# Summing the field products of a tile with two row reductions instead of a tree of six adds

## The reference

```
e = stack of 39 lookups                      # (512, 39, 16), x0 = xk = e
for W in (f0, f1, f2):                       # (39*39, 128), (128*39, 128), (128*39, 128)
    z   = einsum('bfd,bgd->bfgd', x0, xk)    # all products of a field of x0 with a field of xk
    cur = einsum('bpd,pm->bmd', z, W)        # 128 maps
    outs.append(cur); xk = cur
h = concat(sum of each cur over d, dense_ctx)      # 3*128 + 16 numbers
h = relu(h @ W_top1 + b1); h = relu(h @ W_top2 + b2); y = h @ W_top3
```

## Time and profile before

| what | value |
|---|---|
| timed runs | 721.77, 726.46, 728.2 us (median 726.46) |
| profiled execution, its own time (first to last instruction) | 726.1 us |
| PE busy | 686.6 us, 95% |
| DVE busy | 614.4 us, 85% |
| ACT busy | 498.4 us, 69% |
| POOL busy | 255.3 us, 35% |

### The profile page before, as it was taken

One profiled execution on the slowest core, in us unless ns is written; L12 is line 12 of the kernel. 1 busy time (PEld: TensorE's weight loads), 2 busy tenths in 40 slices (PEclk: granted clock), 3 DMA queues, 4 the chain that ended last, 5 costly groups with the idle time before them and its releaser, 6 DMA issues.

```text
span 726.1 us, 12749 instructions
## 1 busy us (share of the span) xinstructions
PE 686.6 (95%) x3569; PEld 495.2 (68%) x3569; DVE 614.4 (85%) x1410; ACT 498.4 (69%) x1663; POOL 255.3 (35%) x247
## 2 busy tenths in 40 slices
PE   3769899999999999999999899999999999999998
PEld 0347567667677877766777687766677787777777
DVE  1638899999999866999999676899999986899990
ACT  2136678778786656878786545877878665787882
POOL 5655628137511707126710702415841000111020
PEclk9969999999999999999999989999999999999999
DMA  7181030303020210202111120020303020030000
GB/s 220 10 278 34 7 86 5 90 2 84 14 75 15 49 46 5 76 14 58 41 52 39 25 65 12 22 71 3 94 4 89 1 63 28 1 89 1 0 2 2
DMA packets 23425, 33.99 MB, mean 47 GB/s; under 512 B 7816, under 2 KB 10616, under 8 KB 22967
## 3 DMA queue, kind: packets, MB, share of 16 engines
q1 hardware_dynamic: 18230, 31.84, 14.4%
q0 software_dynamic: 5120, 1.29, 2.0%
HBM read 9.13 MB, written 0.00 MB: 13 GB/s over the span
## 4 chain that ended last, share of the span: by engine, by line
PE 55%; DVE 21%; issue 11%; ACT 2%; DVEq 1%
DVE sums L683 10%; PE x_ps L920 8%; PE v_ps L776 7%; PE v_ps L778 6%; PE v_ps L777 6%; PE a_ps L776 5%; PE a_ps L778 5%; PE a_ps L777 5%; PE s_ps L890 4%; PE s_ps L979 3%; DVE scaled L626 2%; ACT scaled L452 2%; DVE scaled L616 1%; DVE z_sb L656 1%; DVE sums L672 1%
## 5 line engine op out<-in xcount | busy, mean ns | idle before, releaser
L452 ACT ACTIVATE scaled<-a_ps,x0c 128x128 f32<-128x128 f32 x1216 | 350.3, 379 | 144.0 <-PE a_ps L778 135.8
L683 DVE SCALAR_TENSOR_TENSOR sums<-v_ps,x0c,sums 128x128 f32<-128x128 f32 x768 | 214.8, 341 | 38.4 <-PE v_ps L778 38.4
L776 PE MATMUL v_ps<-w_hi,x_hi 128*128 128x512 f32 x320 | 177.8, 556 | 9.1 <-DVE e_parts L574 4.7
L394 POOL DMA_INDIRECT e_sb<-in_tables,ids_now x140 | 165.6, 1183 | 47.3 <-issue 37.3
L410 POOL TENSOR_TENSOR diag_sb<-x0c,eye_sb 128x320 f32<-128x320 f32 x64 | 61.9, 967 | 329.0 <-PE s_ps L979 328.7
L778 PE MATMUL v_ps<-w_hi,x_lo 128*128 128x512 f32 x320 | 127.6, 399 | 0.0
L777 PE MATMUL v_ps<-w_lo,x_hi 128*128 128x512 f32 x320 | 127.5, 398 | 0.0
L776 PE MATMUL a_ps<-w_hi,x_hi 128*128 128x512 f32 (+1 forms) x320 | 124.5, 389 | 0.0
L777 PE MATMUL a_ps<-w_lo,x_hi 128*128 128x512 f32 (+1 forms) x320 | 123.7, 387 | 0.0
L778 PE MATMUL a_ps<-w_hi,x_lo 128*128 128x512 f32 (+1 forms) x320 | 123.5, 386 | 0.0
L920 PE MATMUL x_ps<-z_sb,w_sb 117*128 117x512 f32 (+1 forms) x210 | 109.5, 602 | 5.9 <-DVE z_sb L656 5.8
(11 more groups left out here) (110 smaller groups left out, 644.9 us busy)
## 6 DMA issues: line engine op xcount, KB each, us to landing
b_sb<-a_sb SPq DMA_DIRECT2D x300, 78.0 KB
w_sb<-in_w SPq DMA_DIRECT2D x1, 2496.0 KB
e_sb<-in_tables,ids_now POOLq DMA_INDIRECT x140
s_sb<-in_w SPq DMA_DIRECT2D x2, 1024.0 KB, 5.3
wt_sb<-in_wt SPq DMA_DIRECT2D x1, 768.0 KB
s_sb<-in_w SPq DMA_DIRECT2D x1, 512.0 KB, 10.5
wt_sb<-in_wt SPq DMA_DIRECT2D x1, 512.0 KB
w_raw<-in_w0a SPq DMA_DIRECT2D x1, 409.5 KB
```

The lines of the kernel that those rows point to most:

```text
L394: pool.indirect_dma_start(out=e_sb[0:rows, i, :], out_offset=None, in_=tables, in_offset=bass.IndirectOffsetOnAxis(ap=ids_now[0:rows, 0, i ...
L452: last = nc.scalar.activation(scaled[:, s % 2, to, j, :], bank[:, j * MAPS:(j + 1) * MAPS], ACT.Copy, scale=x0c[:, k % 4, s, lo + j:lo + j ...
L683: nc.vector.scalar_tensor_tensor(out=sums[:, s % 2, j, :], in0=v_ps[n % 2][:, j * MAPS:(j + 1) * MAPS], scalar=x0c[:, k % 4, s, lo + j:lo ...
L776: nc.tensor.matmul(to, high, w_high, start=True, stop=False)
```

## The change

`scaled` and `sums` become one buffer, `prods`, of 28 rows of 128 maps (for each of two tiles in turn). Rows 0 to 10 hold ACT's products of its last three groups, row 11 an intermediate sum, rows 12 to 15 the four partial sums that DVE accumulates, and rows 16 to 27 ACT's products of the first three groups. The old buffers had 24 and 4 rows, so the size is the same.

The six adds of `sum_tile` go. In their place stand two reductions over rows. `sum_early` runs at group position 4 of the tile itself, and sums rows 12 to 27 (16 rows) into row 11. `sum_late` runs at group position 0 of the next tile, behind line 672, and sums rows 0 to 11 (12 rows) into `x2t`. Both read the buffer as "map outside, row inside", so that consecutive elements of the input lie 128 numbers (512 bytes) apart.

```diff
-LAST_A = A_FIELDS[-1][1] - A_FIELDS[-1][0]
-TAIL = 5
+LATE_AT, EARLY_GROUPS = 0, 3
+EARLY_SUM = LATE_AT + 4 * (SCALED - EARLY_GROUPS) - (4 * GROUPS + 4 * GROUPS - F0)
+SUMS_AT = EARLY_SUM + 1
+EARLY_AT = SUMS_AT + 4
+ROWS = EARLY_AT + 4 * EARLY_GROUPS
+def row_of(group):
+    return EARLY_AT + 4 * group if group < EARLY_GROUPS else LATE_AT + 4 * (group - EARLY_GROUPS)
...
-        scaled = sb("scaled", [128, 2, SCALED, 4, MAPS])
-        sums = sb("sums", [128, 2, 4, MAPS])
+        prods = sb("prods", [128, 2, ROWS, MAPS])
+        sums = prods[:, :, SUMS_AT:SUMS_AT + 4, :]
...
-                    last = nc.scalar.activation(scaled[:, s % 2, to, j, :], bank[:, j * MAPS:(j + 1) * MAPS],
+                    last = nc.scalar.activation(prods[:, s % 2, row_of(to) + j, :], bank[:, j * MAPS:(j + 1) * MAPS],
...
-            def sum_tile(t, k, s, step):
...
+            def sum_rows(out, s, lo, hi):
+                return nc.vector.tensor_reduce(out, prods[:, s % 2, lo:hi, :].rearrange("p r m -> p m r"),
+                                               axis=AX.X, op=ALU.add)
+
+            def sum_early(t, k, s):
+                tile = tile_of(t, k, s)
+                dve.wait_ge(scaled_ready, SCALED * tile + EARLY_GROUPS)
+                dve.wait_ge(macs, mac_count(tile, GROUPS - 2, 3))
+                sum_rows(prods[:, s % 2, EARLY_SUM, :], s, SUMS_AT, ROWS).then_inc(early_summed, 1)
+
+            def sum_late(t, k, s):
+                tile = tile_of(t, k, s)
+                dve.wait_ge(scaled_ready, SCALED * tile + SCALED)
+                dve.wait_ge(early_summed, tile + 1)
+                if not isinstance(t, int) or 4 * t + k >= 2:
+                    dve.wait_ge(s_done, tile - 2 * SUBS + 1)
+                sum_rows(x2t[:, k % 2, s, :], s, LATE_AT, EARLY_SUM + 1).then_inc(x2t_ready, 1)
...
-                    if exists(t, before[0]) and (exists(t, k) or s == 0):
-                        sum_tile(t, before[0], before[1], i)
+                    if not exists(t, k) and s == 0 and i == 0 and exists(t, before[0]):
+                        sum_late(t, before[0], before[1])
...
+                    if i == 0 and exists(t, k) and exists(t, before[0]):
+                        sum_late(t, before[0], before[1])
+                    if i == GROUPS - 1 and exists(t, k):
+                        sum_early(t, k, s)
```

More of the change, by code:

```diff
@@ L237, in dlrm_tower @@
         scaled_ready = sem("scaled_ready")
-        tail_step = sem("tail_step")
+        early_summed = sem("early_summed")
         x2t_ready = sem("x2t_ready")
```

## The result

The changed kernel takes 841.78 us (median of four runs, 839.52 to 842.44) against 727.33 before (median of four runs, one more than the three given above). The ratio is 1.158, with a 95% interval of 1.1545 to 1.1607. Its profiled execution spans 840.0 us, 113.9 more than the 726.1 of before.

What follows compares the result with a forecast made beforehand. DVE was taken to bound the kernel outside three stretches where it waits for PE. The 726.1 us span plus 158 us added DVE work less 33 us hidden in idle time gave 851 us, range 815 to 890.

Steps and rivals of the forecast that it cites:

- DVE bounds outside the three stretches: DVE, 97% busy, sets the pace except at 230-290, 404-460 and 570-630 us, where PE also runs third layer and dense network.
- The step costs 0.68 ns an element, 1.73 in all: Both reductions, reading SBUF 512 bytes apart: 1.05 ns contiguous plus 0.68 for the step, giving 3.69 and 2.80 us.
- rival B: In both reductions a 512-byte step costs more than 128 bytes; doubled extra gives 995 us, half way some 925; chance 8%.
- The reduction as such costs nothing: Line 694's strided reduction from PSUM takes 681 ns, equal to a plain add's 683, so reducing itself adds no cost.
- rival A: Both reductions run at the contiguous rate, 2.3 and 1.75 us; time 720 to 729 us, about 726; chance 12%.
- 0.12 us for the dependence in front of the early reduction: The early reduction waits for the last multiply-add right in front of it, 0.12 us a tile.
- 6.45 us a tile for the two: Both reductions on DVE: 3.69 + 2.80, less 0.16 overlap with the next instruction, plus 0.12 dependence.
- 2.47 us more a tile, 158 in all: DVE's added work: reductions at 6.45 us a tile against 3.98 for the six adds, times 64 tiles.
- 30 us hidden in the three stretches and 3 outside: Added DVE work filling its idle time: 30 of 35 us in the PE-heavy stretches, 3 of 16 us outside.
- 5 us for the coarse order: In the three stretches, large reductions mesh imperfectly with PE, so 30 us are hidden where perfect meshing would hide 35.
- Rival C, the clock: PE's clock falls while it waits for banks; 2 us lost in each of 14 tiles, 28 us, gives 879; chance 8%.

Runs made afterwards that it cites:

- e4: Kernel before, its tree of adds kept, plus five contiguous reductions of 412 zeros a tile, 2.5 us more DVE time a tile; 834.71 us, ratio 1.152.
- e1: Changed kernel with both reductions reading the same rows in memory order, so summing other numbers; 727.79 us, ratio to before 1.0035.
- e2: No kernel: single DVE and ACT instructions alone, at various steps; reductions of 2048 numbers from SBUF took 2.29 us at step 1, 3.57 to 3.81 from step 4.
- e5: No kernel: single DVE and ACT instructions alone, with rows in pairs or fours and small steps; the reduction with pairs took 2.29 us.
- e7: Changed kernel with rows stored in pairs, the two rows' numbers of a map side by side; 727.7 us, ratio 1.0018.
- e8: e7 with each reduction also cut in two over the maps and spread over positions 0 to 3 of the next tile; 720.29 us, ratio 0.991.
- e3: Changed kernel with each strided reduction cut in two over the maps, the four pieces at positions 0 to 3 of the next tile; 837.48 us, ratio 1.154.
- e10: Kernel before with the last two adds of the tree (256 and 128 numbers) moved from DVE to POOL; 757.84 us, ratio 1.043.

## Why the prediction was right

The forecast was 851 us, the range 815 to 890, and 841.78 came. By its steps:

- *DVE bounds outside the three stretches.* Right: e4, with as much DVE work and nothing else of the change, is as slow; the windows show 98%.
- *The step costs 0.68 ns an element, 1.73 in all.* Right in kind, and slightly small: e1 gives 0.74 and 0.72 in the kernel, e2 0.63 alone. The reductions were put at 3.69 and 2.80 us and took 3.79 and 2.85. That the cost doesn't grow beyond 128 bytes was the open bet, and e2 shows it flat to 1024 bytes; rival B is out. The Trainium skill, "Advanced Engine Details and Errata", section "SBUF Cachelines", asks for at least two hits on a 16-byte line. This case agrees: a step of 2 numbers and the pairs, two numbers to a line, take 2.29 us (e2, e5), and a step of 4, one to a line, takes 3.74 (e2).
- *The reduction as such costs nothing* (line 694). Right: 2.29 us contiguous, by 145 + 2048 x 1.05 it should have been 2.30. So rival A's rate is real, and only its layout isn't; e7 is rival A come true by another layout, at 727.7 us.
- *0.12 us for the dependence in front of the early reduction.* Wrong: in 60 of 64 tiles the multiply-add isn't right in front of it, since a `z_sb` product or `x1_lo` stands between (line 656 at 603.80 in the timeline above). Only in the last four tiles does it follow line 683, and there the reduction starts 0.10 us after the end of the multiply-add, where other instructions start 0.08 us before the end of the one ahead:

```profile
802.18 3.30 DVE L683 SCALAR_TENSOR_TENSOR prods<-v_ps,x0c,prods 128x128 f32<-128x128 f32 x12
805.58 3.82 DVE L623 TENSOR_REDUCE prods<-prods 128x128 f32<-128x2048 f32 x1
```

- *6.45 us a tile for the two.* The tile read from start to start shows 6.48, but that is luck: 60 x 0.12 = 7 us that aren't there stand against 64 x 0.15 = 9 us by which the two durations were put too small.
- *2.47 us more a tile, 158 in all.* The tile shows 2.50. The sum over all tiles is 151.9. The term that was too small is the cost of the six adds, taken from one quiet tile: there they are listed with 4.36 us together, and the means over the whole kernel (1232, 1093, 683, 709, 414 and 311 ns) give 4.44, so 5 us more in 64 tiles. `z_sb` also went from 714 to 688 ns, 2 us in its 90 products. The trace of before points to POOL. Line 631 has a median of 680 ns and a longest of 1177. In the two places below it overlaps POOL's `diag_sb` product, and one of the two instructions is stretched, once DVE's and once POOL's, whose median is 0.74 us:

```profile
522.90 0.74 POOL L410 TENSOR_TENSOR diag_sb<-x0c,eye_sb 128x320 f32<-128x320 f32 x1
523.02 1.18 DVE L631 TENSOR_TENSOR sums<-sums,scaled 128x512 f32<-128x512 f32 x1
...
541.49 1.59 POOL L410 TENSOR_TENSOR diag_sb<-x0c,eye_sb 128x320 f32<-128x320 f32 x1 [6.82 <-PE s_ps L979]
541.82 0.68 DVE L631 TENSOR_TENSOR sums<-sums,scaled 128x512 f32<-128x512 f32 x1
```

- *30 us hidden in the three stretches and 3 outside.* In the stretches the idle time fell from 45.1 to 5.0 + 4.6 + 4.1 = 13.7 us, so 31 hidden, and outside from 16 to 9.5, so 6.5. The split is rough, since the stretches of after are cut wider (297 of 1113 instructions of DVE, some 17 tiles, against 14); the sum of 37.9 doesn't hang on it.
- *5 us for the coarse order* (35 us in the stretches, of which 30 are hidden). Somewhat too little: in e7 against e8 the order is worth 7 us of time, and e3 has 9.5 us less idle time than the kernel after. The total of hidden work was nevertheless larger than forecast, 38 us for 33.
- *Rival C, the clock.* PE's waits are there: 45 times for line 683, 73.7 us in all, the longest 2.7 us. The granted clock is 0.95 from 60 to 260 us, so it did fall to the lower level at times. By the windows it cost little or nothing: DVE was busy 98% there. In the last two of the three stretches, where PE had no slack, the clock was 1.00, and in the first it was under that only from 260 to 280 us (0.94), where DVE was busy 19.93 of 20 us. No experiment was made on it.

The profiled span of 840.0 is 11 us under the sum of 851: 6 us because the added work was 151.9 and not 158, and 5 because 38 us of it were hidden and not 33. The timed median lies 1.8 us above that span; in the other runs, too, the time is 1.8 to 1.9 us above the span (730.17 for 728.3 in e1). The prediction took the span for the time and so left out some 2 us. Its 6 and 5 us too much meet these 2 us too little, which is why the median lies only 9 us under 851.

## What to carry to other kernels

Count a reduction by its elements times the rate of its access pattern, not by instructions saved: here 256 instructions fewer cost 114 us. Read the step of the inner index in SBUF; in these runs fp32 at a step of up to 2 numbers, or in pairs of neighbours, was free, and steps of 4 numbers or more cost 60 to 70% more an element in a reduction and were paid on writes too, while reductions from PSUM ran at full rate (0.69 us for 512 numbers at steps of 1 and 32). If two layouts fight, try interleaving by pairs: here both sides then ran at full rate. And where an engine is the bound, spreading its work between the groups of its partner can be worth more than a few fixed costs (7 us here, by e7 and e8).

## What was not expected of the hardware

- An fp32 step of 4 or 8 numbers (3.74 and 3.81 us for 2048) costs more than one of 16 to 256 (3.57 to 3.58), and a step of 2 is free for reads and writes.
- POOL ran faster beside the reductions: its product of 320 numbers fell from a mean of 967 ns before to 737, and its busy time from 255.3 to 209.5 us, though DVE was busier. It isn't the step: with contiguous reductions the product takes 736 ns too (e1), and with the tree of adds kept and contiguous reductions added it takes 1038 (e4). So it goes with DVE's adds and not with how busy DVE is. With two more adds on POOL it was DVE that got slower (e10).
- A strided reduction in the kernel takes 0.2 us longer than alone on the mean (3.79 for 3.58), a contiguous one doesn't. The cause stays open; the trace points to ACT's work beside it (numbers under e2).
